# Expert phase of a gated cross-attention and MoE kernel: turns in two runs of two, up products by token halves, down products two tiles at a time

## The chip, the cores and the metric

One core of one Trainium2 chip. The metric is device time in microseconds (us) of one execution. The median of three runs of the kernel before is 2987.35 us (2986.04 to 2988.27). One more execution was profiled: 2988.55 us.

The engines are named TensorE (PE in the profile; PEld is its weight loads), VectorE (DVE), ScalarE (ACT), GpSimd (POOL) and SyncE (SP). Each runs its own program in order; they meet through semaphores, and a DMA raises its semaphore when it has landed.

## The reference

The input is 4096 tokens of 1024 features. First a layer norm, attention across heads with a context and a gated residual; then a second layer norm and the feed-forward part, in which this change lies:

```python
scores = sigmoid(x_flat @ w_gate)                  # 64 experts
_, topk_idx = top_k(scores, 6)                     # 6 experts per token
w = take(scores, topk_idx); w = w / w.sum(-1)
# each expert takes up to CAP = 512 rows, in token order
x_disp = zeros((E, CAP, C)).at[flat_e, pos].set(x_flat[token_ids], mode='drop')
g_r, v_r = split(einsum('ecd,edh->ech', x_disp, w_up), 2)   # w_up: 64 x 1024 x 256
h_r = silu(g_r) * v_r
out_r = einsum('ech,ehd->ecd', h_r, w_down)                 # w_down: 64 x 128 x 1024
routed = (out_r[flat_e, pos] * w).sum(over the 6)           # plus a shared expert
x = x + tanh(g_ffn) * (shared + routed)
```

All of it in float32. The kernel splits each float32 operand into two float16 parts (hi and lo) and adds three products: hi by hi, hi by lo, lo by hi.

## The kernel before

The program has three phases: attention, routing (which also holds the output projection and the shared expert), and the expert phase `expert_phase`, which is all that the change touches. The routing leaves `rows_dram` (each token's normalized row, hi and lo, 4 KB) and a table with the row number and the weight of each of the 512 places of each expert.

The expert phase goes expert by expert. `steps` calls `step(e, up, down)` on each engine: four experts written out, a loop with two experts per turn, the last two written out, and one step for the last expert's down part. In step e TensorE works on up(e) and then on down(e-1). An expert has 512 rows in four tiles (`TPE = 4`) of 128. The order of the work on each engine is the order in which its program writes it; there is no planner.

GpSimd (`gpsimd_program`): `gather(e+2)` (four indirect DMAs, L1975, one per tile, after an index copy L1971), `weights(e)` (L1987), `add(e-1)` (target copy L2000, then four indirect DMAs, L2008, that add 128 result rows of 4 KB each to `out` in DRAM). Before the target copy, `add` waits until all four adds of the expert before have landed (L1997 to L1999); a row of `out` can be written by several experts.

TensorE (`tensor_program`): `turn(e+1, k)` transposes tile k of the next expert's rows with 32 short products (L2226) into `turn_ps`, which is two PSUM banks and used by every tile in turn. `up_half` (L2231) holds 12 products of 512 columns; four of them, for g and v and the two halves of the contraction, stand between the four turns. g and v have a bank each. `down_tile` (L2243) makes 128 rows by 1024 columns with six products of 512 columns into one of two pairs of banks.

ScalarE and VectorE: `turn` writes the hi part (L2062) and the lo part (L2127) of a turned tile; `split_w` does so for the weights (L2049, L2122; 2048 columns for up, 1024 for down); sigmoid (L2093), gate (L2185) and `multiply` (L2136) make `hidden`; `split_h` (L2055, L2140) splits it. Of each down tile ScalarE evicts the left 512 columns (L2105) and VectorE the right 512 (L2199), both scaled by the row's weight, into `outs`, which has one place per tile; they wait until the add of that tile for the expert before has landed.

SyncE (`load_w`, L1932) loads the next weights, 1.5 MB per expert, once both lo splits of the expert two before are done.

Of the kernel before, what the change touches and what calls it, by code (L numbers as in the profile page):

```python
# [32 lines left out]
P = 128  # L33
# [1786 lines left out]
def expert_phase(nc, ctx, persistent, routing, w_up, w_down, rows_dram, table_dram, out):  # L1820
# [10 lines left out]
    UP, DOWN = 0, 1  # L1831
    part_cols = (slice(0, WU), slice(WU, WU + D))
# [9 lines left out]
    gsig = at(115360, "egsig", [P, CAP], F32)  # L1842
    gated = at(117408, "egated", [P, CAP], F32)
# [13 lines left out]
    with ExitStack() as banks:  # L1857
        def ps(name, shape, dt=F32):
            return banks.enter_context(nc.psum_tensor(name, shape, dt))

        turn_ps = ps("eturn_ps", [P, 2, KC, P // 2])
        g_ps = ps("g_ps", [P, CAP])
        v_ps = ps("v_ps", [P, CAP])

        down_ps = [ps(f"edown_ps{i}", [P, D]) for i in range(2)]

    spare_turn_ps = down_ps[1][:].rearrange("p (h k t) -> p h k t", h=2, k=KC)
# [16 lines left out]
    g_made = sem("g_made")  # L1884
    v_made = sem("v_made")
# [10 lines left out]
    def turned_ps(e, k):  # L1896
        return spare_turn_ps if e.register is None and e.base == 0 and k % 2 else turn_ps[:]
# [4 lines left out]

    def is_last(e):

        return e.register is None and e.base == E - 1

    def outs_of(e):

        if is_last(e):
            return rows[0][:].rearrange("p k d -> p (k d)").bitcast(F32).rearrange("p (k d) -> p k d", k=TPE)  # L1910
        return outs[:]
# [47 lines left out]
    def gpsimd_program(pool):  # L1959
# [30 lines left out]
        def add(e):  # L1990


            if e.register is None and e.base == 0:
                for par in range(2):
                    pool.wait_ge(routed["out_stored"][par], 16 * ((NT - HELD + 1 - par) // 2))
                pool.wait_ge(routed["held_stored"], 16 * HELD)
            for k in range(TPE):  # L1997
                pool.wait_ge(rows_added[k], e.times(16))
                pool.sem_inc(apart, 1)  # L1999
            pool.tensor_copy(target[:], table[:, bass.ds(e.times(TPE), TPE), 0]).then_inc(target_made, 1)  # L2000
            pool.wait_ge(target_made, e.times(1, 1))
            pool.sem_inc(apart, 1)
            for k in range(TPE):
# [6 lines left out]
                    in_=outs_of(e)[:, k, :], in_offset=None, bounds_check=N - 1, oob_is_err=False,  # L2010
# [26 lines left out]
    def scalar_program(act):  # L2037
# [3 lines left out]
        def split_w(e, part):  # L2041
# [3 lines left out]
            if part == UP:  # L2045
                act.wait_ge(v_made, e.times(1, -1))
# [4 lines left out]
        def split_h(e):  # L2051
            act.wait_ge(hidden_made, e.times(1, 1))

            act.wait_ge(down_made, e.times(2 * TPE, -2 * TPE))
            act.activation(h_hi[:, e.base % 2, :], hidden[:], ACT.Copy).then_inc(h_hi_made, 1)  # L2055

        def turn(e, k):
            act.wait_ge(turned, e.times(TPE, k + 1))
            if k == 0:

                act.wait_ge(v_made, e.times(1, -1))
            act.activation(by_half(xt_hi, e, k), turned_ps(e, k).rearrange("p h k t -> p k h t"), ACT.Copy  # L2062
                           ).then_inc(xt_hi_made, 1)

# [15 lines left out]
        def step(e, up, down):  # L2080
            par = e.base % 2
            for k in range(TPE):
                if up and more(e, 1):
                    turn(e.plus(1), k)
                if k == 0 and more(e, 1):
                    split_w(e.plus(1), UP)
                if up and k == 0 and is_last(e):
                    split_w(e, DOWN)
                if up and k == 1:
                    act.wait_ge(g_made, e.times(1, 1))  # L2090

                    act.wait_ge(gated_made, e.times(1))
                    act.activation(gsig[:], g_ps[:], ACT.Sigmoid, scale=1.0 / SCALE).then_inc(gsig_made, 1)  # L2093
                if up and k == 2 and not is_last(e):
                    split_w(e, DOWN)
            if down:
                s = e.plus(-1)
                for k in range(TPE):
                    act.wait_ge(down_made, s.times(2 * TPE, 2 * k + 1))
                    if k == 0:  # L2100
                        act.wait_ge(weight_made, s.times(1, 1))

                    if not is_last(s):
                        act.wait_ge(rows_added[k], s.times(16))
                    act.activation(outs_of(s)[:, k, 0:512], down_ps[k % 2][:, 0:512], ACT.Copy,  # L2105
                                   scale=weight[:, s.base % 2, k:k + 1]
                                   ).then_inc(left_kept, 1)
                    if up and k == 0 and not is_last(e):
                        split_h(e)
            if up and (not down or is_last(e)):  # L2110
                split_h(e)
# [3 lines left out]
    def vector_program(dve):  # L2115
# [9 lines left out]
        def turn(e, k):  # L2125
            dve.wait_ge(xt_hi_made, e.times(TPE, k + 1))
            dve.tensor_tensor(by_half(xt_lo, e, k), turned_ps(e, k).rearrange("p h k t -> p k h t"),  # L2127
                              by_half(xt_hi, e, k), ALU.subtract).then_inc(xt_lo_made, 1)

        def multiply(e):  # L2130

            dve.wait_ge(v_made, e.times(1, 1))
            dve.wait_ge(gated_made, e.times(1, 1))

            dve.wait_ge(h_lo_made, e.times(1))
            dve.tensor_tensor(hidden[:], gated[:], v_ps[:], ALU.mult).then_inc(hidden_made, 1)  # L2136

        def split_h(e):
            dve.wait_ge(h_hi_made, e.times(1, 1))
            dve.tensor_tensor(h_lo[:, e.base % 2, :], hidden[:], h_hi[:, e.base % 2, :], ALU.subtract  # L2140
                              ).then_inc(h_lo_made, 1)
# [31 lines left out]
        def step(e, up, down):  # L2173
            par = e.base % 2
            for k in range(TPE):
                if up and more(e, 1):
                    turn(e.plus(1), k)
                if k == 1 and more(e, 1):
                    split_w(e.plus(1), UP)
                if up and k == 1 and is_last(e):  # L2180
                    split_w(e, DOWN)
                if up and k == 2:
                    dve.wait_ge(gsig_made, e.times(1, 1))

                    dve.scalar_tensor_tensor(gated[:], g_ps[:], 1.0 / SCALE ** 2, gsig[:],  # L2185
                                             ALU.mult, ALU.mult).then_inc(gated_made, 1)
                    if not is_last(e):
                        split_w(e, DOWN)
            if up and not is_last(e):
                multiply(e)  # L2190
            if down:
                s = e.plus(-1)
                for k in range(TPE):
                    dve.wait_ge(down_made, s.times(2 * TPE, 2 * k + 2))
                    if k == 0:
                        dve.wait_ge(weight_made, s.times(1, 1))
                    if not is_last(s):
                        dve.wait_ge(rows_added[k], s.times(16))
                    dve.tensor_scalar(outs_of(s)[:, k, 512:D], down_ps[k % 2][:, 512:D],  # L2199
                                      weight[:, s.base % 2, k:k + 1], None, ALU.mult  # L2200
                                      ).then_inc(right_kept, 1)
                    if up and k == 1 and not is_last(e):
                        split_h(e)
            if up and is_last(e):
                multiply(e)
            if up and (not down or is_last(e)):
                split_h(e)
        steps(dve, first, step)

    def tensor_program(pe):  # L2210
# [3 lines left out]
        def turn(e, k):  # L2214
# [6 lines left out]
            pe.wait_ge(xt_lo_made, max(k - 1, 0) if first else e.times(TPE, k))  # L2221
            for c in range(KC):
                for w in range(2):
                    for h in range(2):
                        half = slice(h * P // 2, (h + 1) * P // 2)
                        last = pe.matmul(turned_ps(e, k)[:, h, c, :],  # L2226
# [4 lines left out]
        def up_half(e, part, half):  # L2231
            par = e.base % 2
            out = (g_ps, v_ps)[part][:]
            for c in range(half * KC // 2, (half + 1) * KC // 2):
                at = c * 2 * HR + part * HR
                wh, wl = (w[:, par, at:at + HR] for w in (w_hi, w_lo))
                pe.matmul(out, wh, xt_hi[par][:, c, :], start=(c == 0), stop=False)  # L2237
                pe.matmul(out, wh, xt_lo[par][:, c, :], start=False, stop=False)  # L2238
                last = pe.matmul(out, wl, xt_hi[par][:, c, :], start=False, stop=(c == KC - 1))  # L2239
            if half == 1:  # L2240
                last.then_inc((g_made, v_made)[part], 1)

        def down_tile(s, k):  # L2243
            par = s.base % 2
            if k == 0 and s.register is None and s.base == 0:

                pe.wait_ge(routed["result_made"], NT)
            for half, kept in ((0, left_kept), (1, right_kept)):

                pe.wait_ge(kept, s.times(TPE, k - 1))  # L2250
# [117 lines left out]
```

## Time and profile before

| | |
|---|---|
| median of three runs | 2987.35 us (2986.04 to 2988.27) |
| profiled execution | 2988.55 us, of which its span 2986.6 us, granted clock 0.993 |
| TensorE products | 2921.6 us busy, 98% of the span |
| VectorE | 2204.2 us, 74% |
| ScalarE | 1360.0 us, 46% |
| GpSimd | 1428.0 us, 48% |
| all DMA | 509.92 MB, mean 171 GB/s |

The span runs from the first to the last instruction. The expert phase begins some 1800 us into it. In a time row of the profile come the start, the length, engine, line, operation, out<-in, how many, and in brackets the idle time of the engine before it and what ended that. Products on TensorE overlap: their length is not their spacing, which is read from their starts.

### The profile page before, as it was taken

The page shows a single profiled execution, that of the slowest core. Times are in us where ns is not written, and L with a number is a line of the kernel's source. Part 1 is how long each engine was busy: PE and PEld are TensorE (multiplying, and loading weights), DVE is VectorE, ACT ScalarE, POOL GpSimd, SP SyncE. Part 2 cuts the span into 40 slices and gives each one's busy share as a digit, 9 for nine tenths or more (in the row PEclk, how much of TensorE's full clock was granted, in tenths as well). Part 3 has the DMA queues.
Part 4 walks back from the last instruction along what each step waited for, and adds up shares of the span by engine and source line. Part 5 has one row for each costly group of instructions (what it writes and reads, how often), then busy time and mean ns, then how long its engine had stood idle before and what let it go on. Part 6 is the DMA issues. An engine that isn't in the chain of part 4 may idle for free.

```text
span 2986.6 us, 75019 instructions
## 1 busy us (share of the span) xinstructions
PE 2921.6 (98%) x27408; PEld 1705.4 (57%) x27408; DVE 2204.2 (74%) x3786; ACT 1360.0 (46%) x2201; POOL 1428.0 (48%) x1326
## 2 busy tenths in 40 slices
PE   8999999999999998999999999999999999999997
PEld 6777777777777764444444444444444444444443
DVE  7777777777777777777777767776777777777774
ACT  7444444444444454111111115555555555555553
POOL 4222222222222213455555565777777777677774
PEclk9999999999999999999999999999999999999998
DMA  6333443333333335544445556899999999999996
GB/s 236 93 99 87 106 101 97 89 86 86 90 86 88 95 106 174 142 140 139 130 132 141 153 152 204 242 259 260 249 248 266 248 257 270 262 270 278 266 271 129
DMA packets 371543, 509.92 MB, mean 171 GB/s; under 512 B 234446, under 2 KB 267214, under 8 KB 363168
## 3 DMA queue, kind: packets, MB, share of 16 engines
q1 hardware_dynamic: 291488, 305.97, 33.7%
q0 software_dynamic: 79872, 201.48, 28.3%
q8 instruction: 119, 1.95, 0.3%
q14 instruction: 64, 0.52, 0.1%
HBM read 340.27 MB, written 201.79 MB: 181 GB/s over the span
## 4 chain that ended last, share of the span: by engine, by line
PE 92%; DVE 3%; issue 2%; POOL 1%; ACT 1%; DMA 0%; SPq 0%; POOLq 0%; DVEq 0%; ACTq 0%
PE proj_ps L922 7%; PE proj_ps L924 7%; PE proj_ps L923 7%; PE eturn_ps L2226 5%; PE v_ps L2237 4%; PE g_ps L2237 4%; PE edown_ps L2254 4%; PE edown_ps L2255 4%; PE edown_ps L2256 4%; PE v_ps L2239 4%; PE v_ps L2238 4%; PE g_ps L2239 4%; PE g_ps L2238 4%; PE proj_ps L968 4%; PE proj_ps L970 3%; PE proj_ps L969 3%
## 5 line engine op out<-in xcount | busy, mean ns | idle before, releaser
L2008 POOL DMA_INDIRECT out<-outs,target x252 | 399.2, 1584 | 218.0 <-ACT outs L2105 160.0
L2127 DVE TENSOR_TENSOR ext_lo<-eturn_ps,ext_hi 128x1024 f16<-128x1024 f32 x254 | 310.7, 1223 | 201.1 <-ACT ext_hi L2062 200.9
L1975 POOL DMA_INDIRECT rows<-rows_dram,index x256 | 389.2, 1520 | 118.2 <-POOL index L1971 59.6
L2062 ACT ACTIVATE ext_hi<-eturn_ps 128x1024 f16<-128x1024 f32 x254 | 260.2, 1024 | 143.6 <-PE eturn_ps L2226 143.0
L922 PE MATMUL proj_ps<-ct_hi,wk_wv_hi 128*128 128x256 f16 x1008 | 275.9, 274 | 9.3 <-DVE wk_wv_lo L763 9.3
L922 PE MATMUL proj_ps<-xt,wq_wo_hi 128*128 128x256 f16 x1008 | 275.5, 273 | 1.3 <-DVE whole L737 1.0
L2105 ACT ACTIVATE outs<-edown_ps,weight 128x512 f32<-128x512 f32 x252 | 173.2, 688 | 226.8 <-PE edown_ps L2256 225.8
L923 PE MATMUL proj_ps<-ct_lo,wk_wv_hi 128*128 128x256 f16 x1008 | 275.7, 274 | 0.0
L924 PE MATMUL proj_ps<-ct_hi,wk_wv_lo 128*128 128x256 f16 x1008 | 275.6, 273 | 0.0
L923 PE MATMUL proj_ps<-xt,wq_wo_hi 128*128 128x256 f16 x1008 | 275.2, 273 | 0.0
L924 PE MATMUL proj_ps<-xt,wq_wo_lo 128*128 128x256 f16 x1008 | 275.1, 273 | 0.0
L2199 DVE TENSOR_SCALAR outs<-edown_ps,weight 128x512 f32<-128x512 f32 x252 | 189.1, 751 | 104.4 <-PE edown_ps L2256 104.4
L589 ACT ACTIVATE whole<-proj_ps,bias 64x128 f32<-64x128 f32 x504 | 180.9, 359 | 169.0 <-PE proj_ps L924 162.8
L499 POOL TENSOR_TENSOR sc<-sc,neg_max 128x256 f32<-128x256 f32 x64 | 40.1, 627 | 441.1 <-DVE neg_max L783 441.0
L1347 POOL DMA_INDIRECT table_dram<-record,entry x192 | 207.6, 1081 | 75.7 <-issue 49.3
L2122 DVE SCALAR_TENSOR_TENSOR ew_lo<-ew_in,ew_hi 128x2048 f16<-128x2048 f32 (+1 forms) x128 | 223.9, 1749 | 0.4 <-ACT ew_hi L2049 0.4
L737 DVE TENSOR_SCALAR whole<-proj_ps,bias 64x128 f32<-64x128 f32 x496 | 176.5, 356 | 62.1 <-PE proj_ps L924 50.5
L1712 PE MATMUL o_ps<-wq_wo_hi,at_hi 128*128 128x512 f16 x512 | 194.6, 380 | 8.4 <-DVE y_held L1637 4.5
L2254 PE MATMUL edown_ps<-ew_hi,h_hi 128*128 128x512 f16 x512 | 194.8, 381 | 2.2 <-DVE h_lo L2140 2.2
L2237 PE MATMUL g_ps<-ext_hi,ew_hi 128*128 128x512 f16 x512 | 195.4, 382 | 0.0
L2237 PE MATMUL v_ps<-ext_hi,ew_hi 128*128 128x512 f16 x512 | 195.4, 382 | 0.0
L2226 PEld LDWEIGHTS eturn_ps<-squares,rows 64*128 64x128 f16 x8128 | 132.8, 95 | 108.7 <-DVE ext_lo L2127 74.1
(257 smaller groups left out, 7345.7 us busy)
## 6 DMA issues: line engine op xcount, KB each, us to landing
ew_in<-w_up SPq DMA_DIRECT2D x64, 1024.0 KB
ew_in<-w_down SPq DMA_DIRECT2D x64, 512.0 KB
x_in<-x SPq DMA_DIRECT2D x16, 1024.0 KB, 5.7
v_dram<-vt SPq DMA_DIRECT2D x64, 256.0 KB, 2.1
late<-v_dram SPq DMA_DIRECT2D x32, 512.0 KB, 7.4
attn_dram<-attn SPq DMA_DIRECT2D x64, 256.0 KB, 2.0
a_in<-attn_dram SPq DMA_DIRECT2D x32, 512.0 KB, 3.8
rx_in<-x SPq DMA_DIRECT2D x32, 512.0 KB, 4.1
```

The costliest lines, as they stand in the source:

```text
L922: pe.matmul(out, wh, hi[:, k, :], start=(k == 0), stop=False)
L923: pe.matmul(out, wh, lo[:, k, :], start=False, stop=False)
L924: last = pe.matmul(out, wl, hi[:, k, :], start=False, stop=(k == KC - 1))
L1975: pool.indirect_dma_start(out=rows[par][:, k, :], out_offset=None, in_=rows_dram, in_offset=bass.IndirectOffsetOnAxis(ap=index[:, par, k:k ...
L2008: pool.indirect_dma_start(out=out, out_offset=bass.IndirectOffsetOnAxis(ap=target[:, k:k + 1], axis=0), in_=outs_of(e)[:, k, :], in_offset ...
L2062: act.activation(by_half(xt_hi, e, k), turned_ps(e, k).rearrange("p h k t -> p k h t"), ACT.Copy).then_inc(xt_hi_made, 1)
L2127: dve.tensor_tensor(by_half(xt_lo, e, k), turned_ps(e, k).rearrange("p h k t -> p k h t"), by_half(xt_hi, e, k), ALU.subtract).then_inc(xt ...
L2226: last = pe.matmul(turned_ps(e, k)[:, h, c, :], rows[par][half, k, w * D + c * P:w * D + (c + 1) * P], squares[half], start=(w == 0), stop ...
L2237: pe.matmul(out, wh, xt_hi[par][:, c, :], start=(c == 0), stop=False)
L2238: pe.matmul(out, wh, xt_lo[par][:, c, :], start=False, stop=False)
L2239: last = pe.matmul(out, wl, xt_hi[par][:, c, :], start=False, stop=(c == KC - 1))
L2254: pe.matmul(to, hh, w_hi[:, par, cols], start=True, stop=False)
```

## The change

- GpSimd's `add` is cut in two. In step e it issues adds 2 and 3 of expert e-1, and then adds 0 and 1 of expert e. The wait for the landing of all adds of the expert before, and the target copy, stand in the first half (tiles 0 and 1).
- The turns of the next expert come in two runs of two tiles. There are two turn buffers (`turn_ps[k % 2]`), so a turn waits for the lo part of the tile two before.
- The up products go by token halves: 256 columns each, g and v of one half beside each other in one bank `gv_ps`; a half's products wait until `hidden` of the half before is made. Sigmoid, gate, multiply and `split_h` work on halves too.
- The down products of two tiles follow each half: `down_half(e-1, 1)` behind `up_half(e, 0)`, `down_half(e, 0)` behind `up_half(e, 1)`. They use three banks of 512 columns; the fourth unit of a half takes the bank of its first.
- The last expert's special order and its separate result buffer are gone.
- On ScalarE and VectorE the order follows TensorE's: turns 0 and 1, down split, gate of half 0, evictions 2 and 3 of the expert before, turns 2 and 3, up split, gate of half 1, evictions 0 and 1.

```diff
 # GpSimd
-        def add(e):
+        def add(e, half):
...
-            for k in range(TPE):
-                pool.wait_ge(rows_added[k], e.times(16))
+            if half == 0:
+                for k in range(TPE):
+                    pool.wait_ge(rows_added[k], e.times(16))
+                    pool.sem_inc(apart, 1)
+                pool.tensor_copy(target[:], table[:, bass.ds(e.times(TPE), TPE), 0]).then_inc(target_made, 1)
+                pool.wait_ge(target_made, e.times(1, 1))
                 pool.sem_inc(apart, 1)
-            pool.tensor_copy(target[:], table[:, bass.ds(e.times(TPE), TPE), 0]).then_inc(target_made, 1)
-            pool.wait_ge(target_made, e.times(1, 1))
-            pool.sem_inc(apart, 1)
-            for k in range(TPE):
+            for k in range(2 * half, 2 * half + 2):
                 pool.wait_ge(left_kept, e.times(TPE, k + 1))
...
 # GpSimd, step (gather(e + 2) and weights(e) stand above)
             if down:
-                add(e.plus(-1))
+                add(e.plus(-1), 1)
+            if up:
+                add(e, 0)
 # TensorE
-            pe.wait_ge(xt_lo_made, max(k - 1, 0) if first else e.times(TPE, k))
+            pe.wait_ge(xt_lo_made, e.times(TPE, k - 1))
...
+        def up_half(e, half):
+            par = e.base % 2
+            pe.wait_ge(xt_lo_made, e.times(TPE, 2 * half + 2))
+
+            pe.wait_ge(hidden_made, e.times(2, half))
+            hi, lo = (xt[par][:, :, tokens(half)] for xt in (xt_hi, xt_lo))
+            for part in range(2):
+                for c in range(KC):
+                    cols = slice(c * 2 * HR + part * HR, c * 2 * HR + (part + 1) * HR)
+                    wh, wl = (w[:, par, cols] for w in (w_hi, w_lo))
+                    pe.matmul(gv_ps[:, part], wh, hi[:, c, :], start=(c == 0), stop=False)
+                    pe.matmul(gv_ps[:, part], wh, lo[:, c, :], start=False, stop=False)
+                    last = pe.matmul(gv_ps[:, part], wl, hi[:, c, :], start=False, stop=(c == KC - 1))
+            last.then_inc(gv_made, 1)
+
+        def down_half(s, tiles):
...
+            pe.wait_ge(left_kept, s.times(TPE, first))
+            pe.wait_ge(right_kept, s.times(TPE, first))
+            for k in range(first, first + 2):
+                for right, part in ((0, LEFT), (1, RIGHT)):
+                    if k == first + 1 and right:
+
+                        pe.wait_ge(left_kept, s.times(TPE, first + 1))
...
         def step(e, up, down):
             if up:
+                if more(e, 1):
+                    turn(e.plus(1), 0)
+                    turn(e.plus(1), 1)
                 pe.wait_ge(w_lo_made[UP], e.times(1, 1))
...
+                up_half(e, 0)
+            if down:
+                down_half(e.plus(-1), 1)
+            if up:
+                if more(e, 1):
+                    turn(e.plus(1), 2)
+                    turn(e.plus(1), 3)
+                up_half(e, 1)
+                down_half(e, 0)
```

## Rows read from the trace of the kernel before

**Rows 1.** The page's chain that ended last: shares of the span by engine.
```profile
PE 92%; DVE 3%; issue 2%; POOL 1%; ACT 1%; DMA 0%; SPq 0%; POOLq 0%; DVEq 0%; ACTq 0%
```

**Rows 2.** Stretch table: stretch, its us, busy us by engine (instructions), clock, DMA share, GB/s.
```profile
2383.00:2438.00 55.00, 55.00 (x603) 26.54 (x601) 38.92 (x39) 32.49 (x37) 39.35 (x34) 1.00 0.90 248
```

**Rows 3.** Timeline, TensorE: one turn between up products.
```profile
2399.80 0.38 PE L2239 MATMUL g_ps<-ext_hi,ew_lo 128*128 128x512 f16 x1
...
2400.12 0.64 PE L2226 MATMUL eturn_ps<-squares,rows 64*128 64x64 f16 x32
...
2400.69 0.39 PE L2237 MATMUL g_ps<-ext_hi,ew_hi 128*128 128x512 f16 x1
```

**Rows 4.** Timeline, TensorE, attention: first and last of 49 products of 256 columns.
```profile
800.58 0.27 PE L923 MATMUL proj_ps<-xt,wq_wo_hi 128*128 128x256 f16 x1
...
805.82 0.27 PE L923 MATMUL proj_ps<-ct_lo,wk_wv_hi 128*128 128x256 f16 x1
```

**Rows 5.** Timeline, GpSimd: one round of adds and gathers in the loop.
```profile
2394.84 1.62 POOL L2008 DMA_INDIRECT out<-outs,target  x1 [2.44 <-ACT outs L2105]
2396.76 1.60 POOL L2008 DMA_INDIRECT out<-outs,target  x1 [0.30 <-DVE outs L2199]
...
2400.54 1.56 POOL L2008 DMA_INDIRECT out<-outs,target  x1 [0.30 <-issue]
2401.51 0.79 POOL L1971 CAST index<-table 128x4 int32 x1
2403.23 3.03 POOL L1975 DMA_INDIRECT rows<-rows_dram,index  x1 [0.93 <-POOL index L1971]
...
2410.34 0.19 POOL L1987 COPY weight<-table 128x4 f32 x1
2410.48 0.18 POOL L2000 CAST target<-table 128x4 int32 x1
2413.09 1.62 POOL L2008 DMA_INDIRECT out<-outs,target  x1 [2.43 <-ACT outs L2105]
```

**Rows 6.** Timeline, TensorE: two turns in a row ahead of the first expert.
```profile
1783.27 0.64 PE L2226 MATMUL eturn_ps<-squares,rows 64*128 64x64 f16 x32
1783.74 0.63 PE L2226 MATMUL edown_ps<-squares,rows 64*128 64x64 f16 x32
1784.31 0.39 PE L1712 MATMUL up_ps<-up_hi,yt 128*128 128x512 f16 x1
```

**Rows 7.** Timeline: the third product of a down unit, and its eviction.
```profile
2410.26 0.38 PE L2256 MATMUL edown_ps<-ew_hi,h_lo 128*128 128x512 f16 x1
...
2410.76 0.69 ACT L2105 ACTIVATE outs<-edown_ps,weight 128x512 f32<-128x512 f32 x1 [2.39 <-PE edown_ps L2256]
```

**Rows 8.** Timeline, GpSimd, last experts; then all adds' time to landing (L2008).
```profile
2961.76 1.55 POOL L2008 DMA_INDIRECT out<-outs,target  x1 [0.30 <-issue]
2967.90 0.19 POOL L2000 CAST target<-table 128x4 int32<-128x4 f32 x1 [4.59 <-DMA out<-outs,target]
...
2974.73 1.55 POOL L2008 DMA_INDIRECT out<-rows,target  x1 [0.30 <-issue]
...
DMA to landing us min/median/max: 6.7/8.5/10.3
```

**Rows 9.** Timeline, GpSimd: index copy, first gather and weight copy in an early step.
```profile
1808.86 0.71 POOL L1971 CAST index<-table 128x4 int32<-128x4 f32 x1 [8.74 <-PE eturn_ps L2226]
1810.46 1.02 POOL L1975 DMA_INDIRECT rows<-rows_dram,index  x1 [0.88 <-POOL index L1971]
...
1815.67 0.19 POOL L1987 COPY weight<-table 128x4 f32<-128x4 f32 x1
```

**Rows 10.** Timeline, VectorE: split of the up weights beside the gather of rows 5.
```profile
2403.01 2.28 DVE L2122 SCALAR_TENSOR_TENSOR ew_lo<-ew_in,ew_hi 128x2048 f16<-128x2048 f32 x1
```

**Rows 11.** Stretch table near the end, columns as in rows 2.
```profile
2960.00:2964.00 4.00, 1.83 (x9) 0.71 (x8) 1.38 (x2) 1.20 (x2) 3.01 (x2) 0.98 1.05 202
2964.00:2968.00 4.00, 4.00 (x13) 1.46 (x12) 1.50 (x2) 1.10 (x3) 0.10 (x1) 0.59 0.73 134
```

More of the change, by code:

```diff
@@ L1859, in ps @@
             return banks.enter_context(nc.psum_tensor(name, shape, dt))
[L1861 to L1867, printed above, removed]
+        even_turn_ps = ps("even_turn_ps", [P, 2, KC, P // 2])
+        first_down_ps = ps("first_down_ps", [P, 512])
+        gv_ps = ps("gv_ps", [P, 2, HALF])
+        late_down_ps = [ps(f"late_down_ps{i}", [P, 512]) for i in range(2)]
+        odd_turn_ps = ps("odd_turn_ps", [P, 2, KC, P // 2])
+    turn_ps = [even_turn_ps, odd_turn_ps]
+    down_ps = [first_down_ps] + late_down_ps
     table_landed = sem("table_landed")
@@ L1894, in expert_phase, with down_unit, tokens @@
     rows_added = [sem(f"rows_added{k}") for k in range(TPE)]
-    def turned_ps(e, k):
-        return spare_turn_ps if e.register is None and e.base == 0 and k % 2 else turn_ps[:]
+    def down_unit(k, right):
+        return down_ps[(2 * (k % 2) + right) % 3]
+    def tokens(half):
+        return slice(half * HALF, (half + 1) * HALF)
     def by_half(of, e, k):
         return of[e.base % 2][:, :, k * P:(k + 1) * P].rearrange("p k (h t) -> p k h t", h=2)
[L1903 to L1911, printed above, removed]
     def more(e, ahead):
@@ L1988, in weights @@
                              ).then_inc(weight_made, 1)
-        def add(e):
-            if e.register is None and e.base == 0:
+        def add(e, half):
+            if half == 0 and e.register is None and e.base == 0:
                 for par in range(2):
@@ L2059, in turn, with sigmoid, keep @@
             if k == 0:
-                act.wait_ge(v_made, e.times(1, -1))
-            act.activation(by_half(xt_hi, e, k), turned_ps(e, k).rearrange("p h k t -> p k h t"), ACT.Copy
+                act.wait_ge(gv_made, e.times(2, -2))
+            act.activation(by_half(xt_hi, e, k), turn_ps[k % 2][:].rearrange("p h k t -> p k h t"), ACT.Copy
                            ).then_inc(xt_hi_made, 1)
+        def sigmoid(e, half):
+            act.wait_ge(gv_made, e.times(2, half + 1))
+            act.wait_ge(gated_made, e.times(2, half))
+            act.activation(gsig[:], gv_ps[:, 0], ACT.Sigmoid, scale=1.0 / SCALE).then_inc(gsig_made, 1)
+        def keep(e, k):
+            act.wait_ge(down_made, e.times(2 * TPE, 2 * k + 1))
+            if k == 0:
+                act.wait_ge(weight_made, e.times(1, 1))
+            act.wait_ge(rows_added[k], e.times(16))
+            act.activation(outs[:, k, LEFT], down_unit(k, 0)[:], ACT.Copy,
+                           scale=weight[:, e.base % 2, k:k + 1]).then_inc(left_kept, 1)
         def first():
@@ L2080, in step @@
         def step(e, up, down):
[L2081 to L2085, printed above, removed]
-                    split_w(e.plus(1), UP)
[L2087 to L2111, printed above, removed]
+            if up:
+                if more(e, 1):
+                    turn(e.plus(1), 0)
+                    turn(e.plus(1), 1)
+                split_w(e, DOWN)
+                sigmoid(e, 0)
+            if down:
+                keep(e.plus(-1), 2)
+            if up:
+                split_h(e, 0)
+            if down:
+                keep(e.plus(-1), 3)
+            if up:
+                if more(e, 1):
+                    turn(e.plus(1), 2)
+                    turn(e.plus(1), 3)
+                    split_w(e.plus(1), UP)
+                sigmoid(e, 1)
+                keep(e, 0)
+                split_h(e, 1)
+                keep(e, 1)
         steps(act, first, step)
@@ L2126, in turn, with multiply, split_h, keep @@
             dve.wait_ge(xt_hi_made, e.times(TPE, k + 1))
-            dve.tensor_tensor(by_half(xt_lo, e, k), turned_ps(e, k).rearrange("p h k t -> p k h t"),
+            dve.tensor_tensor(by_half(xt_lo, e, k), turn_ps[k % 2][:].rearrange("p h k t -> p k h t"),
                               by_half(xt_hi, e, k), ALU.subtract).then_inc(xt_lo_made, 1)
[L2130 to L2141, printed above, removed]
+        def multiply(e, half):
+            dve.wait_ge(gsig_made, e.times(2, half + 1))
+            dve.scalar_tensor_tensor(gated[:], gv_ps[:, 0], 1.0 / SCALE ** 2, gsig[:],
+                                     ALU.mult, ALU.mult).then_inc(gated_made, 1)
+            dve.wait_ge(gated_made, e.times(2, half + 1))
+            dve.wait_ge(h_lo_made, e.times(2, half - 1))
+            dve.tensor_tensor(hidden[:, tokens(half)], gated[:], gv_ps[:, 1], ALU.mult).then_inc(hidden_made, 1)
+        def split_h(e, half):
+            dve.wait_ge(h_hi_made, e.times(2, half + 1))
+            dve.tensor_tensor(h_lo[:, e.base % 2, tokens(half)], hidden[:, tokens(half)],
+                              h_hi[:, e.base % 2, tokens(half)], ALU.subtract).then_inc(h_lo_made, 1)
+        def keep(e, k):
+            dve.wait_ge(down_made, e.times(2 * TPE, 2 * k + 2))
+            if k == 0:
+                dve.wait_ge(weight_made, e.times(1, 1))
+            dve.wait_ge(rows_added[k], e.times(16))
+            dve.tensor_scalar(outs[:, k, RIGHT], down_unit(k, 1)[:], weight[:, e.base % 2, k:k + 1], None, ALU.mult
+                              ).then_inc(right_kept, 1)
         def clear_rows(par):
@@ L2173, in step @@
         def step(e, up, down):
[L2174 to L2178, printed above, removed]
-                    split_w(e.plus(1), UP)
[L2180 to L2207, printed above, removed]
+            if up:
+                if more(e, 1):
+                    turn(e.plus(1), 0)
+                    turn(e.plus(1), 1)
+                split_w(e, DOWN)
+                multiply(e, 0)
+            if down:
+                keep(e.plus(-1), 2)
+            if up:
+                split_h(e, 0)
+            if down:
+                keep(e.plus(-1), 3)
+            if up:
+                if more(e, 1):
+                    turn(e.plus(1), 2)
+                    turn(e.plus(1), 3)
+                    split_w(e.plus(1), UP)
+                multiply(e, 1)
+                keep(e, 0)
+                split_h(e, 1)
+                keep(e, 1)
         steps(dve, first, step)
@@ L2229, in turn @@
             last.then_inc(turned, 1)
-        def up_half(e, part, half):
+        def up_half(e, half):
             par = e.base % 2
[L2233 to L2241, printed above, removed]
@@ L2275, in first @@
             shared_down(held[-1])
-        def down_all(s):
-            pe.wait_ge(h_lo_made, s.times(1, 1))
-            pe.wait_ge(w_lo_made[DOWN], s.times(1, 1))
-            for k in range(TPE):
-                down_tile(s, k)
         def step(e, up, down):
             if up:
+                if more(e, 1):
+                    turn(e.plus(1), 0)
+                    turn(e.plus(1), 1)
                 pe.wait_ge(w_lo_made[UP], e.times(1, 1))
-                pe.wait_ge(xt_lo_made, e.times(TPE, TPE))
-                pe.wait_ge(hidden_made, e.times(1))
-                for part in range(2):
-                    for half in range(2):
-                        if more(e, 1):
-                            turn(e.plus(1), 2 * part + half)
-                        up_half(e, part, half)
-                    if part == 0 and is_last(e):
-                        down_all(e.plus(-1))
-            if down and not is_last(e):
-                down_all(e.plus(-1))
+                up_half(e, 0)
+            if down:
+                down_half(e.plus(-1), 1)
+            if up:
+                if more(e, 1):
+                    turn(e.plus(1), 2)
+                    turn(e.plus(1), 3)
+                up_half(e, 1)
+                down_half(e, 0)
         steps(pe, first, step)
```

42 lines of the change are left out of this document (21 added, 21 removed).

## The prediction

> **What bounds the kernel now.** I read the page's chain of waits first: TensorE carries 92% of it [rows 1]. Then the table of stretches: in three experts' time TensorE is busy 55.00 of 55 us at full clock, VectorE 38.92, ScalarE 32.49, GpSimd 39.35, and the DMA engines 0.90 of the stretch [rows 2]. So the expert phase runs at TensorE's pace, one expert every 18.25 us (the first add of an expert at 2394.84, that of the next at 2413.09, [rows 5]). TensorE's share is 72 products of 512 columns and four turns of 32 short ones. A turn costs 0.68: from the product that starts before it (2399.80) to the one after it (2400.69) are 0.89 [rows 3], less the product itself; (18.25 - 4 x 0.68) / 72 gives 0.215 for that one.
>
> GpSimd is busy, but with slack: it writes four adds, four gathers, copies the next targets at 2410.48 without waiting, and then stands 2.43 us for ScalarE's eviction [rows 5]. The adds of one expert must have landed before the next expert's targets are copied (L1997 to L2000), and before, the four gathers lie between, so that the landing is hidden. That is the place to watch.
>
> **The change on TensorE.** Turns two at a time: two neighbours took from 1783.27 to 1784.31, 1.04, with the second's start 0.47 behind the first's [rows 6]; with the 0.11 that a turn loses on entry (2399.80 + 0.215 to 2400.12, [rows 3]) a pair costs 1.15 instead of 1.36, so 0.42 less per expert. Up products: 48 of 512 columns become 96 of 256. Those of the attention phase follow each other every (805.82 - 800.58) / 48 = 0.109 [rows 4], so 96 take 10.48 against 48 x 0.215 = 10.32: 0.16 more. The 24 down products keep their size. Sum: 0.26 less, 17.99 us per expert of TensorE; over 62 experts 16 us, which by itself would give 2988.55 - 16 = 2972. The cover for this: up products of a half need xt_lo of that half, made a step earlier; the one gv bank is reused after 12 down products and two turns, some 3.7 us, in which sigmoid, two multiplies and the waits fit (a 512-wide eviction takes 0.69, [rows 7]).
>
> The fourth down unit of each half reuses the first one's bank. ScalarE started evicting at 2410.76, 0.50 behind the start of the unit's third product, and took 0.69 [rows 7]; the fourth unit starts seven products, 1.51, behind that third one, so 0.3 is left. If ScalarE is on time this costs nothing; if an operation of about its own length (0.69) is in front, it costs 0.4 per half.
>
> ScalarE and VectorE get the same columns in twice the instructions for sigmoid, gate, multiply and splits. Their price is the fixed part of five instructions each at most; even 0.3 us for each would make VectorE 38.92/3 + 1.5, about 14.5, and ScalarE less [rows 2]. Both stay below 18. SyncE's weight loads are only released earlier, because the down split moves ahead of the up products. I cost these edits at nothing. The end of the run loses the special order of the last expert; a few us either way.
>
> **The change on GpSimd.** One step was: gather four tiles for two experts ahead, weight copy, [wait for the older adds], target copy, four adds. It becomes: gather four, weight copy, adds 2 and 3 of expert e-1, **wait until all adds of e-1 have landed**, target copy, adds 0 and 1 of e. The number of instructions is the same. But the wait for the landing now stands directly behind the add it waits for. GpSimd works in order, so behind that wait stand the target copy, two adds and the next four gathers, and nothing else can go on. The loop closes on GpSimd alone:
> - add 2 to add 3: 1.92 (2394.84 to 2396.76, [rows 5]);
> - add 3 to the target copy released by its landing: near the end, where no gather fills the queue, 6.14 (2961.76 to 2967.90, [rows 8]); over the adds whose landing the profile tells the least is 6.7, the median 8.5, the most 10.3 [rows 8]. After the change only one add is ahead and the weight loads fall elsewhere, but four gathers are in front: I take 6.7, the low end under way;
> - target copy to add 0: 0.19 + 0.88, as index copy to gather, with the target copy's own length [rows 8, 9]: 1.07;
> - add 0 to add 1: 1.92;
> - add 1 to the index copy: 0.97 (2400.54 to 2401.51, [rows 5]);
> - index copy to the end of the weight copy, with four gathers: 2401.51 to 2410.34 + 0.19 = 9.02 [rows 5], or 1808.86 to 1815.67 + 0.19 = 7.00 in the first step [rows 9]. The difference is the first gather, 3.03 against 1.02: it began 0.22 behind VectorE's 2.28 us split of the up weights and ended 0.97 after that [rows 10]. The four gathers start over 6 us, and once per expert this split will fall on one of them again; I take 9.02;
> - to add 2: 0.30.
>
> Sum: 1.92 + 6.7 + 1.07 + 1.92 + 0.97 + 9.02 + 0.30 = **21.90 us per expert**, against TensorE's 17.99. Bounds: 6.14 and 7.00 give 19.32; 8.5 and 9.02 give 23.70; 10.3 and 9.02 give 25.50. TensorE and the evictions don't lengthen this loop: their results for adds 2 and 3 are ready some 9 us into TensorE's step, and TensorE can start a step as soon as the gathers of the round before have landed, so it is early and then waits for gathers (its first wait in the new trace should be there).
>
> The Trainium skill, page "DMA: Bandwidth & Descriptors", section "Anatomy of one DMA — SWDGE (gpsimd) path", puts a transfer at about 2.0 us plus its bytes over 436 GB/s. For an add of 512 KB behind 1.55 us of descriptor writing this would be an estimated 4.75 us instead of 6.7, and with 7.00 for the gathers a loop of 17.9, no longer than TensorE's. The trace disagrees: 6.14 is what an add took with next to nothing beside it [rows 8].
>
> **The whole.** The first round's add 2: the last turn of the first step released the index copy at 1808.86 [rows 9]; by the sums above that is 36 products and four turns, 10.5 us, into the step, so the step began at 1798.3. The new one: 12.8 us of turns and up products, two down units 1.3, an eviction with its wait 0.97: first add at 1813.4; then 1.92 + 0.97 + 9.02 + 0.30 gives 1825.6. Sixty rounds of P follow (to expert 61, the last gather), then three rounds without gathers, 1.92 + 6.7 + 1.07 + 1.92 + 1.57 + 0.5 = 13.7 each, 1.92 to the last add, and from its start to the end of the span 2986.6 - 2974.73 = 11.87 [rows 8]: 54.9. Outside the span are 2988.55 - 2986.6 = 1.95. Time = 1825.6 + 54.9 + 1.95 + 60 P = 1882.5 + 60 P; with P = 21.90 it is **3196 us**. This is set against the profiled 2988.55, which is 1.2 above the median of the runs, nothing beside these sizes. The kernel breaks even at P = 18.4.
>
> **Rivals.**
> - *The loop is tighter*: no gather is caught by a VectorE split. P = 19.32 to 19.88 (6.14 or 6.7): 3042 to 3075. For it: in the first step no gather was caught [rows 9]. Against it: the split recurs once per expert and gathers take a third of the loop. Slower too, by half as much.
> - *The landing stays hidden and TensorE still bounds*: 2972, faster. It needs P below 18, so a landing under 4.8 even without a caught gather; no row shows one. The estimate from the Trainium skill's page "DMA: Bandwidth & Descriptors" above is of this size.
> - *Banks of the down products*: GpSimd is not the bound, but ScalarE comes late to the first unit's eviction in each half. Price 0.4 x 2 x 62 = 50 on top of 2972: 3022, slower; it decides once ScalarE is over 0.3 late, and turns into gain below 0.13 of loss per half.
> - *TensorE's clock*: near the end the clock fell after a stretch in which TensorE was busy 1.83 of 4 us, and was 0.59 over the next four [rows 11], a loss of 4 x 0.41 = 1.6 us. In the new kernel TensorE would idle 3.9 per expert. One such loss makes its step 19.6, two 21.2, still below 21.90, so it takes slack and no time; with several falls per expert it could join the bound at about 24 (3320).
>
> **How the numbers follow.** Forecast (3110 to 3310, P from 20.5 to 23.8) 0.65; tighter loop (3030 to 3110) 0.19; loaded landings or clock (above 3310) 0.09; banks alone 0.02; TensorE still the bound 0.05, of which 0.01 lies within 0.2% (what a measurement here can tell from no change). Range 3045 to 3310. Faster 0.04, same 0.01, slower 0.95.
>
> **What would show it.** Right: GpSimd's target copy waits several us for the adds' landing once per expert; TensorE's idle time ahead of turns is put down to gathers; TensorE busy about 82% of a stretch; rows of the target copy 21 to 23 us apart. TensorE's own step, where undisturbed, should hold pairs of turns in 1.15 and up products every 0.109. Wrong: target copies without idle time before them, or experts every 18 us; then landings are far shorter than any seen, or another engine reaches the wait so late that it hides them.

## The result, and the profile after

The changed kernel takes 3124.82 us (median of four runs, 3109.84 to 3131.70) against 2987.72 for the kernel before (four runs): a ratio of 1.0451, interval 1.0431 to 1.0471. It is slower, as forecast. The forecast of 3196 us was 71 too long. The profiled execution took 3109.84 us, with a span of 3108.1.

First the page's chain of waits of the changed kernel, as in [rows 1]:

```profile
PE 55%; DMA 18%; issue 12%; POOL 8%; DVE 3%; POOLq 1%; ACT 1%; SPq 0%; DVEq 0%; ACTq 0%
DMA out<-outs,target 17%; PE proj_ps L922 7%; PE proj_ps L923 7%; PE proj_ps L924 7%; POOL out L2006 4%; PE proj_ps L968 3%; PE proj_ps L969 3%; PE proj_ps L970 3%; PE o_ps L1712 3%; PE o_ps L1713 3%; PE o_ps L1714 3%; POOL rows L1972 2%; PE up_ps L1712 2%; PE up_ps L1713 2%; PE up_ps L1714 2%
```

TensorE's share fell from 92% to 55%, and the new second is a DMA: the adds into `out`. The expert phase has left TensorE's chain almost entirely; the TensorE lines shown belong to the phases before it.

Who waited for whom, over the whole changed kernel (waiter <- releaser: us in total, times, longest):

```profile
POOL target L1998 <- DMA out<-outs,target: 267.2, 63, 6.4
...
ACT outs L2077 <- POOL weight L1984: 145.8, 56, 5.1
...
PEld first_down_ps L2268 <- ACT outs L2077: 129.7, 56, 4.8
...
PE first_down_ps L2268 <- ACT outs L2077: 102.2, 56, 4.3
```

The first line is the forecast's wait: the target copy waits once per expert for the landing of the adds. The other three are a wait that the forecast did not name, looked at below.

GpSimd's timeline over two rounds, to be laid beside [rows 5]:

```profile
2351.28 1.62 POOL L2006 DMA_INDIRECT out<-outs,target  x1 [0.17 <-issue]
2353.21 1.60 POOL L2006 DMA_INDIRECT out<-outs,target  x1 [0.30 <-issue]
2361.17 0.19 POOL L1998 CAST target<-table 128x4 int32 x1 [6.37 <-DMA out<-outs,target]
2362.48 1.58 POOL L2006 DMA_INDIRECT out<-outs,target  x1 [1.12 <-ACT outs L2077]
2364.36 1.57 POOL L2006 DMA_INDIRECT out<-outs,target  x1 [0.30 <-issue]
2365.35 0.78 POOL L1968 CAST index<-table 128x4 int32 x1
2367.07 1.08 POOL L1972 DMA_INDIRECT rows<-rows_dram,index  x1 [0.94 <-POOL index L1968]
2368.46 2.46 POOL L1972 DMA_INDIRECT rows<-rows_dram,index  x1 [0.31 <-issue]
2371.22 1.00 POOL L1972 DMA_INDIRECT rows<-rows_dram,index  x1 [0.30 <-issue]
2372.52 1.00 POOL L1972 DMA_INDIRECT rows<-rows_dram,index  x1 [0.30 <-issue]
2373.53 0.19 POOL L1984 COPY weight<-table 128x4 f32 x1
2373.89 1.62 POOL L2006 DMA_INDIRECT out<-outs,target  x1 [0.17 <-issue]
2375.82 1.57 POOL L2006 DMA_INDIRECT out<-outs,target  x1 [0.30 <-issue]
2380.43 0.23 POOL L1998 CAST target<-table 128x4 int32 x1 [3.04 <-DMA out<-outs,target]
...
1911.57 0.49 POOL L1998 CAST target<-table 128x4 int32 x1 [3.44 <-DMA out<-outs,target]
...
2937.72 0.19 POOL L1998 CAST target<-table 128x4 int32 x1 [3.92 <-DMA out<-outs,target]
```

Where a row of [rows 5] had no idle time before the target copy, here are 6.37 and 3.04 us. The copy at 1911.57 and that at 2937.72 are 50 rounds apart: 20.52 us per expert. Put into the forecast's formula, 1882.5 + 60 x 20.52 is 3114, against 3109.84 for this execution.

TensorE over a long stretch (columns as in [rows 2]):

```profile
2000.00:2900.00 900.00, 811.52 (x10805) 600.12 (x10804) 592.82 (x699) 468.63 (x611) 548.15 (x480) 0.98 0.87 231
```

It is busy 90% instead of all of the time. VectorE, ScalarE, GpSimd and the DMA engines are all less busy per us than in [rows 2]. No engine is saturated, as in a loop that waits for a latency; the experiments test this.

### The profile page after: what moved, and what is told of

Same layout as the page of the kernel before. It is cut to its first block, busy times and chain, and to the rows that moved or that the text cites. A ratio compares the mean times of both kernels' runs of the same rounds, so it can differ in the third digit from the quotient of the medians.

```text
span 3108.1 us, 81965 instructions
## 1 busy us (share of the span) xinstructions
PE 2936.0 (94%) x30480; PEld 2018.8 (65%) x30480; DVE 2241.6 (72%) x3978; ACT 1364.4 (44%) x2329; POOL 1399.0 (45%) x1326
## 3 DMA queue, kind: packets, MB, share of 16 engines
q0 software_dynamic: 79872, 201.48, 27.3%
## 4 chain that ended last, share of the span: by engine, by line
PE 55%; DMA 18%; issue 12%; POOL 8%; DVE 3%; POOLq 1%; ACT 1%; SPq 0%; DVEq 0%; ACTq 0%
DMA out<-outs,target 17%; PE proj_ps L922 7%; PE proj_ps L923 7%; PE proj_ps L924 7%; POOL out L2006 4%; PE proj_ps L968 3%; PE proj_ps L969 3%; PE proj_ps L970 3%; PE o_ps L1712 3%; PE o_ps L1713 3%; PE o_ps L1714 3%; POOL rows L1972 2%; PE up_ps L1712 2%; PE up_ps L1713 2%; PE up_ps L1714 2%
## 5 line engine op out<-in xcount | busy, mean ns | idle before, releaser
L2244 PE MATMUL gv_ps<-ext_hi,ew_hi 128*128 128x256 f16 x2048 | 565.1, 276 | 0.4 <-DVE ehidden L2143 0.4
L2245 PE MATMUL gv_ps<-ext_lo,ew_hi 128*128 128x256 f16 x2048 | 563.6, 275 | 0.0
L2246 PE MATMUL gv_ps<-ext_hi,ew_lo 128*128 128x256 f16 x2048 | 563.0, 275 | 0.0
L2006 POOL DMA_INDIRECT out<-outs,target x256 | 409.9, 1601 | 130.1 <-issue 101.4
L1972 POOL DMA_INDIRECT rows<-rows_dram,index x256 | 345.9, 1351 | 118.2 <-POOL index L1968 59.6
L2132 DVE TENSOR_TENSOR ext_lo<-even_turn_ps,ext_hi 128x1024 f16<-128x1024 f32 x128 | 156.8, 1225 | 124.5 <-ACT ext_hi L2062 124.5
L2244 PEld LDWEIGHTS gv_ps<-ext_hi,ew_hi 128*128 128x128 f16 x2048 | 202.0, 99 | 31.2 <-issue 0.5
L2246 PEld LDWEIGHTS gv_ps<-ext_hi,ew_lo 128*128 128x128 f16 x2048 | 202.4, 99 | 25.3
L2245 PEld LDWEIGHTS gv_ps<-ext_lo,ew_hi 128*128 128x128 f16 x2048 | 202.3, 99 | 23.5
L2069 ACT ACTIVATE egsig<-gv_ps 128x256 f32<-128x256 f32 x128 | 49.2, 384 | 342.7 <-PE gv_ps L2246 342.7
```

The source lines that it names most:

```text
L1972: pool.indirect_dma_start(out=rows[par][:, k, :], out_offset=None, in_=rows_dram, in_offset=bass.IndirectOffsetOnAxis(ap=index[:, par, k:k ...
L2006: pool.indirect_dma_start(out=out, out_offset=bass.IndirectOffsetOnAxis(ap=target[:, k:k + 1], axis=0), in_=outs[:, k, :], in_offset=None, ...
L2244: pe.matmul(gv_ps[:, part], wh, hi[:, c, :], start=(c == 0), stop=False)
L2245: pe.matmul(gv_ps[:, part], wh, lo[:, c, :], start=False, stop=False)
L2246: last = pe.matmul(gv_ps[:, part], wl, hi[:, c, :], start=False, stop=(c == KC - 1))
```

## Experiments

Each kernel differs from the changed one (or, in the second, from the one before) by the edit shown. Ratios are to the kernel before, run on the same chip.

**All four adds together again.** GpSimd's step of the changed kernel, with both halves of the adds behind the gathers:

```diff
             if down:
+                add(e.plus(-1), 0)
                 add(e.plus(-1), 1)
-            if up:
-                add(e, 0)
```

> The changed kernel with GpSimd's order of before: in step e, after the gathers and the weight copy, the target copy and all four adds of expert e-1; nothing else differs. Theory (the landing of adds 2 and 3 stands uncovered in GpSimd's round of 20.5 us): the gathers cover the landing again, GpSimd's round falls to 3 x 1.9 + 1.0 + 8.2 + 1.6, about 16.5 us, TensorE bounds with 17.99 per expert, and the time is about 2972 us (2960 to 2985). Rival (the cost comes from TensorE's new order: halves, one bank for g and v, three banks for down products): the time stays above 3050.

Measured: 2965.64 us, ratio 0.9925 (0.9906 to 0.9945). That is 159 us less than the changed kernel for the order of three calls, and 0.75% less than before. Rounds, from two of its target copies 50 rounds apart, and one pair of turns on TensorE:

```profile
1902.79 0.18 POOL L1998 CAST target<-table 128x4 int32 x1
...
2804.95 0.19 POOL L1998 CAST target<-table 128x4 int32 x1 [0.41 <-DMA out<-outs,target]
...
2384.54 0.38 PE L2269 MATMUL first_down_ps<-ew_hi,h_lo 128*128 128x512 f16 x1
2384.85 0.64 PE L2228 MATMUL even_turn_ps<-squares,rows 64*128 64x64 f16 x32
2385.33 0.63 PE L2228 MATMUL odd_turn_ps<-squares,rows 64*128 64x64 f16 x32
2385.89 0.28 PE L2243 MATMUL gv_ps<-ext_hi,ew_hi 128*128 128x256 f16 x1
...
2391.03 0.27 PE L2245 MATMUL gv_ps<-ext_hi,ew_lo 128*128 128x256 f16 x1
```

902.16 / 50 is 18.04 us per expert, where TensorE's sum gave 17.99; a pair of turns costs 2385.89 - 2384.54 - 0.215 = 1.14, where 1.15 was worked out. The last two rows are the first and last of the 48 up products of a half: (2391.03 - 2385.89) / 47 is 0.109, as forecast. So the TensorE half of the change works as meant, and the whole loss sits in GpSimd's order. The rival of late evictions at the three banks falls with it: this kernel has the same banks and takes 2965.64 us, not 3022.

**The same wait in the kernel before.** Behind `add(e-1)`:

```diff
                 add(e.plus(-1))
+                for k in range(TPE):
+                    pool.wait_ge(rows_added[k], e.times(16))
+                    pool.sem_inc(apart, 1)
```

> The kernel before, with one wait more on GpSimd: behind the four adds of an expert it waits until they have landed, before the next gathers. No transfer and no product differs. Theory: GpSimd's round becomes 3 x 1.9 + 6.3 (landing) + 7.9 (index copy, gathers, weight copy) + 1.4, about 21.3 us, and bounds; 60 x (21.3 - 18.25) is 183 us more, about 3170 us (3080 to 3260). Rival (GpSimd's wait is covered by other slack, the loss in the changed kernel is of its halves): about 2988 us.

Measured: 3198.31 us, ratio 1.0699 (1.0680 to 1.0719). One wait alone, without halves, pairs or banks, makes the old kernel even slower than the changed one. Its GpSimd timeline:

```profile
2386.14 1.55 POOL L2008 DMA_INDIRECT out<-outs,target  x1 [0.30 <-issue]
2395.19 0.19 POOL L1971 CAST index<-table 128x4 int32 x1 [7.50 <-issue]
...
2408.52 2.04 POOL L2008 DMA_INDIRECT out<-outs,target  x1 [0.30 <-issue]
2417.20 0.67 POOL L1971 CAST index<-table 128x4 int32 x1 [6.64 <-DMA out<-outs,target]
```

In these two rounds 9.05 and 8.68 lie between the start of the last add and the next index copy, not the 6.3 expected. The profile names no releaser for the first of these waits; its place is the new wait's. Over the run (us, times, longest) the two entries are:

```profile
POOL index L1971 <- issue: 178.6, 28, 10.1
POOL index L1971 <- DMA out<-outs,target: 172.1, 30, 9.9
```

That is (178.6 + 172.1) / 58 = 6.05 per round, where the changed kernel's target copy waits 267.2 / 63 = 4.24: the last of four adds lands later than the second of two. The direction and the mechanism held, the size was 28 us short.

**The gathers between the halves.** The adds stay cut in two, but the gathers move from ahead of them to between them:

```diff
-            if more(e, 2):
-                gather(e.plus(2))
             if up:
                 weights(e)
             if down:
                 add(e.plus(-1), 1)
+            if more(e, 3):
+                gather(e.plus(3))
             if up:
                 add(e, 0)
```

(The gathers of expert 2 are issued ahead of the first step, and GpSimd's loop ends two experts earlier, so that none is asked for beyond the last.)

> The changed kernel with its adds in halves, but the gathers of expert e+3 moved from the start of step e+1 to between the adds 2 and 3 of expert e-1 and the target copy of expert e, in the same order of waits otherwise. Theory: the gathers cover the landing, GpSimd's round falls to about 16.5 us, TensorE bounds: about 2972 us (2960 to 2990). Rival (adds in halves cost time by themselves, by more waits or by worse DMA order): above 3050 us.

Measured: 2967.09 us, ratio 0.9930 (0.9911 to 0.9949). So adds in halves cost nothing. What costs is that no gathers stand between the last add of one expert and the wait of the next. One round of it, and the wait over the run:

```profile
2397.19 1.58 POOL L2006 DMA_INDIRECT out<-outs,target  x1 [0.51 <-ACT outs L2086]
2399.28 1.55 POOL L2006 DMA_INDIRECT out<-outs,target  x1 [0.51 <-issue]
...
2407.45 1.00 POOL L1972 DMA_INDIRECT rows<-rows_dram,index  x1 [0.30 <-issue]
2408.45 0.20 POOL L1998 CAST target<-table 128x4 int32 x1
2409.82 1.62 POOL L2006 DMA_INDIRECT out<-outs,target  x1 [1.17 <-issue]
...
POOL target L1998 <- DMA out<-outs,target: 70.6, 44, 8.8
```

The target copy at 2408.45 comes straight behind the last gather, 9.17 after the start of the last add, and has no wait left in this round. In other rounds it still waits, but for 70.6 us in all instead of 267.2.

**The weight copy first.** In the changed kernel ScalarE's first eviction waits for GpSimd's weight copy, which stands behind four gathers, and TensorE's fourth down unit waits for that eviction.

```diff
-            if more(e, 2):
-                gather(e.plus(2))
             if up:
                 weights(e)
+            if more(e, 2):
+                gather(e.plus(2))
```

> The changed kernel with the weight copy ahead of the gathers in GpSimd's step. In the changed kernel's trace ScalarE's eviction waits 145.8 us in all for that copy, and TensorE waits for ScalarE. Theory (GpSimd's round bounds, TensorE's waits lie in its slack): that wait goes, the time stays at 3125 us within 20. Rival (the late weight copy is the cause): faster by 60 to 145 us.

Measured: 3135.74 us, ratio 1.0484 (1.0461 to 1.0507), not faster; the intervals overlap with the changed kernel's, so the 11 us between them are not told apart. Its waits:

```profile
POOL target L1998 <- DMA out<-outs,target: 286.0, 63, 7.5
...
PE even_turn_ps L2229 <- DMA rows<-rows_dram,index: 65.3, 45, 3.2
...
PE odd_turn_ps L2229 <- DMA rows<-rows_dram,index: 57.1, 54, 2.7
```

The wait for the weight copy is gone from the list, and TensorE now waits for the gathers instead, the place that the forecast named. A wait of 145.8 us was removed and bought nothing: it stood in slack.

**The split of the up weights in four.** In VectorE's `split_w`:

```diff
-            dve.scalar_tensor_tensor(w_lo[w], w_in[w], SCALE, w_hi[w], ALU.mult, ALU.subtract
-                                     ).then_inc(w_lo_made[part], 1)
+            cols = part_cols[part]
+            pieces = 4 if part == UP else 1
+            wide = (cols.stop - cols.start) // pieces
+            for i in range(pieces):
+                w = (slice(None), e.base % 2, slice(cols.start + i * wide, cols.start + (i + 1) * wide))
+                last = dve.scalar_tensor_tensor(w_lo[w], w_in[w], SCALE, w_hi[w], ALU.mult, ALU.subtract)
+            last.then_inc(w_lo_made[part], 1)
```

> The changed kernel with VectorE's lo split of the up weights in four instructions of 512 columns instead of one of 2048 (2.28 us). Theory: GpSimd's round bounds and each of its terms counts in full; in it one gather per expert takes 2.3 to 2.9 us instead of 1.0 because that split runs beside it. With pieces of 0.6 us the gather loses at most that, the round falls by some 0.8, and the time by 60 x 0.8: about 3075 us (3050 to 3110). Rival (that term is covered, or the gather waits for something else): 3125 us within 15.

Measured: 3086.51 us, ratio 1.0321 (1.0304 to 1.0339), 38 us less than the changed kernel. The gathers' group and the wait for the landing, first in the changed kernel, then with the split in four (gathers: busy us, mean ns | idle before; wait: us, times, longest), both from the expert phase:

```profile
L1972 POOL DMA_INDIRECT rows<-rows_dram,index x244 | 329.4, 1350 | 112.8 <-POOL index L1968 56.9 <-issue 53.1 <-DMA out<-outs,target 2.1
```

```profile
L1972 POOL DMA_INDIRECT rows<-rows_dram,index x244 | 274.7, 1126 | 112.8 <-POOL index L1968 56.9 <-issue 52.5 <-DMA out<-outs,target 2.7
...
POOL target L1998 <- DMA out<-outs,target: 296.4, 63, 6.7
```

The gathers lost 54.7 us, the wait for the landing grew by 296.4 - 267.2 = 29.2, which leaves 25.5; the spans of the two profiled executions differ by 3108.1 - 3085.7 = 22.4. (The 38 us are between medians; the changed kernel's profiled execution, 3109.84, is 15 us below its median.) So this term does count, and a part of it comes back as a later landing. Why the adds land later there was not tried.

**The same split where GpSimd does not bound**, with all four adds together:

> The changed kernel with all four adds together behind the gathers (2966 us in its own run), and VectorE's lo split of the up weights in four instructions. Theory: GpSimd no longer bounds, so what a caught gather loses costs nothing: 2966 us within 6. Rival (GpSimd is still part of the bound): faster by 15 us or more.

Measured: 2966.78 us, ratio 0.9922 (0.9905 to 0.9938), no different from 2965.64. The same edit is worth 38 us in one kernel and nothing in the other.

**Ten more products per expert on TensorE**, ahead of each half's up products, in the changed kernel and in the one with all four adds together:

```diff
+            for again in range(5):
+                pe.matmul(gv_ps[:, 0], w_hi[:, par, 0:HR], hi[:, 0, :], start=True, stop=True)
             for part in range(2):
```

> The changed kernel with ten more products of 256 columns per expert on TensorE (five ahead of each half's up products, overwritten by them): 10 x 0.109 = 1.09 us per expert. Theory: TensorE has some 2.7 us of slack per round of GpSimd, the time stays at 3125 us within 20. Rival (TensorE with its waits is what bounds): 62 x 1.09 = 67 us more, about 3190 us.

Measured in the changed kernel: 3134.55 us, ratio 1.0481 (1.0463 to 1.0498); 10 us more, with overlapping intervals, instead of 67.

> The changed kernel with all four adds together behind the gathers (2966 us in its own run) and the same ten more products per expert. Theory: with the landing covered TensorE bounds, so all 67 us show: about 3033 us (3020 to 3045). Rival (GpSimd or the DMA engines, 0.94 busy, still set the pace): below 2995 us.

Measured with the adds together: 3032.15 us, ratio 1.0140 (1.0123 to 1.0157), 66.5 us more than without. So 67 us of TensorE's work are nearly free in one kernel and fully paid in the other: TensorE does not bound the changed kernel and does bound the repaired one.

## Why the prediction was right

The step that decided was right: the wait for the adds' landing had been covered by the gathers, the change puts it straight behind the adds it waits for, and GpSimd's in-order round then becomes longer than TensorE's. Two sizes in the sum were off, both upwards, and one place. The measured round lies at the lower end of the 20.5 to 23.8 that the forecast allowed: one gather per round was slowed as supposed, but the landing was shorter.

- *The round*: 21.90 forecast, 20.52 measured. From the rows after: add 2 to add 3 1.93 (1.92 forecast); target copy to add 0 1.31 (1.07); add to add 1.88 (1.92); add to index copy 0.99 (0.97); weight copy's end to add 2 0.17 (0.30). Together these add 0.10; with landing and gathers, below, 0.10 - 0.85 - 0.65 is -1.40, against 20.52 - 21.90 = -1.38.
- *Landing*: 6.7 forecast. The two rounds shown have 2361.17 - 2353.21 = 7.96 and 2380.43 - 2375.82 = 4.61. The others vary likewise; over 63 rounds the copy waited 267.2 / 63 = 4.24, and add 3's own 1.6 us before that make about 5.85. The forecast was 0.85 too much. The low bound, 6.14, came from the last of four adds in a row [rows 8], and here only one add stands ahead. That 6.14 was called an add with next to nothing beside it; [rows 11] show the DMA engines at 1.05 and 0.73 over those us.
- *What an add moves*: the description of the kernel and the forecast took every add for 128 rows of 4 KB. Here are GpSimd's DMA queue (packets, MB, share) over the whole run of the changed kernel, and then in the two rounds shown, from the start of add 2 to the target copy:

```profile
q0 software_dynamic: 79872, 201.48, 27.3%
...
q0 software_dynamic: 613, 1.51, 65.9%
...
q0 software_dynamic: 603, 0.71, 58.0%
```

256 gathers and 256 adds of 128 rows of 4 KB would be 268 MB. But 4096 tokens with 6 experts each fill only 24576 of the 32768 places; moved twice, these rows are 201.3 MB. The kernel gives an empty place a row number beyond the last token (L1370), and its row is not moved. The places fill in order, so the empty ones lie in an expert's last tiles, which are adds 2 and 3, ahead of the wait. In the round with 7.96 the queue moved 1.51 MB, in that with 4.61 only 0.71, remainders of the gathers included, where two full adds alone are 1.05. The estimate of 4.75 from the Trainium skill, page "DMA: Bandwidth & Descriptors", section "Anatomy of one DMA — SWDGE (gpsimd) path", was worked out for 512 KB, so the round with 4.61 does not bear it out, and the mean of 5.85 is above it. That no row shows a landing under 4.8 held for the kernel before.
- *Gathers*: 9.02 forecast; in the round shown 2373.53 + 0.19 - 2365.35 = 8.37. The caught gather takes 2.46 instead of the 3.03 of [rows 5]: it began at 2368.46, 0.74 behind the start of VectorE's split, where that of [rows 10] began 0.22 behind. In 56 of the run's last 62 groups of four gathers one took over 1.5 us, so nearly every round has a slowed one, as supposed, and the split in four bears it out.

```profile
2367.72 2.29 DVE L2127 SCALAR_TENSOR_TENSOR ew_lo<-ew_in,ew_hi 128x2048 f16<-128x2048 f32 x1 [0.35 <-ACT ew_hi L2049]
```

- *TensorE's side*: 17.99 per expert forecast, 18.04 where it bounds; 2972 us forecast for that case, 2965.64 measured.
- *A rival's price*: the tighter loop was called slower by half as much. Its 3042 to 3075 are 53 to 86 us above 2988.55, a quarter to two fifths of the forecast's 207.
- *Clock*: the fall was foreseen and did not set the time, since TensorE has slack here (ten more products cost 10 of 67 us). In this stretch table of the changed kernel TensorE is busy 0.18 of 3.10 us, and the granted clock of the next two stretches is 0.73 and 0.50. The last is the lower of the clock's two levels, 1.2 of 2.4 GHz:

```profile
2348.90:2352.00 3.10, 0.18 (x2) 0.04 (x2) 0.69 (x1) 0.78 (x2) 2.62 (x4) 1.00 0.93 315
2352.00:2354.00 2.00, 2.00 (x57) 1.46 (x59) 1.23 (x3) 1.06 (x3) 1.70 (x2) 0.73 0.97 273
2354.00:2356.00 2.00, 2.00 (x26) 1.48 (x21) 1.21 (x2) 2.00 (x3) 0.80 (x1) 0.50 1.03 190
```

- *Wrong in detail*: TensorE's idle time was to be ahead of turns, put down to gathers. It stands ahead of the fourth down unit:

```profile
2351.22 0.69 ACT L2077 ACTIVATE outs<-first_down_ps,weight 128x512 f32<-128x512 f32 x1 [3.70 <-POOL weight L1984]
...
2351.97 0.39 PE L2268 MATMUL first_down_ps<-ew_hi,h_hi 128*128 128x512 f16 x1 [2.92 <-ACT outs L2077]
```

The evictions of an expert's first tiles now come half a step earlier, in the step in which its weights are copied, and that copy stands behind the gathers. The forecast followed the evictions' waits for banks and landings and passed over this one. It cost nothing only because GpSimd's round was longer still. TensorE's share was also given as 82%; it is 90%, since a shorter round and the stretches at the lower clock fill it.

Open: the landing varies by over 3 us from round to round in one execution. The two rounds shown differ in the rows that the queue moved; no run changed that number, so how much of the variation it makes is not shown.

## What to carry to other kernels

When work on an in-order queue is cut and reordered, look for the waits that had been covered by what stood between: the count of instructions can stay the same and the round still grow by a whole latency. Add up the round of every engine's queue, with each wait in it, not only of the engine that bounds now. Here the cure keeps the halves and moves the gathers between the last add and the wait: 2967 us, with all the gain on TensorE.

## What the runs showed of the hardware that was not expected

An add's landing is not one number. In the kernel before it was 6.7 to 10.3 us where the profile tells it [rows 8]; in the changed one, over all adds, as short as 3.2:

```profile
DMA to landing us min/median/max: 3.2/7.1/11.8
```

Where GpSimd waits for a landing and issues nothing more, two adds came in 4.61 and 7.96 us after the second's start in the rounds shown, and in the kernel with four adds ahead of the wait 8.68 and 9.05 us after the fourth's. A latency read from a busy queue is then only roughly the one that a kernel which waits for it will pay; nor does an add always move its 128 rows, as the queue's 201.48 MB instead of 268 show.
